# The first store of a pairwise product kernel: issued behind most of the head's loads, or when its products are finished

## The chip, the cores and the metric

The kernel runs on one core of a Trainium2 chip. The metric is the device time of one execution in microseconds (us). The inputs are laid out and the outputs put back in order by the host, which isn't timed.

## The reference

```python
def _L0_rec_ref(x, W):                      # x: 4096 x 32 x 64, W: 64 x 64, float32
    vid = jnp.einsum('bfd,de->bfe', x, W)
    F_ = x.shape[1]
    idx_i, idx_j = jnp.triu_indices(F_, k=1)
    return x[:, idx_i, :] * vid[:, idx_j, :]  # 4096 x 496 x 64
```

For every sample, the 32 fields are multiplied by one matrix, and for each of the 496 pairs of fields i < j the row of field i is multiplied element by element with the transformed row of field j. 33.6 MB go in and 520 MB come out.

## The kernel before

**Tiles and units.** Two halves of the batch lie on the 128 partitions (2 x 64 embedding places), so a tile holds 256 samples: 128 columns for each of 32 fields. There are 16 tiles. All data in on-chip memory stands in one tensor `mem` of 445 units; a unit is 128 columns of float32 on 128 partitions, 64 KB. A tile of x is 32 units, its products are 496 units.

**Work on a tile.** TensorE multiplies the 32 fields by a block diagonal matrix made of W twice (`w2`), in two halves of 16 fields (first fields 16 to 31, then 0 to 15), into `vid`, which fills the PSUM. VectorE then forms the products (L295, `tensor_tensor` with mult), up to 128 pairs in one instruction, from `mem` and `vid` into `mem`. When a half of `vid` is used up it tells TensorE through the semaphore `free`.

**Slots.** The 16 x 496 product units are cut into 74 slots (`SLOTS`), each with a number of units and a home in `mem` where it is gathered, and is then written to `out` by one DMA (`store`, issued through `transfer`, L192). Slots lie over each other and over x data that has been used, so a product instruction waits until the stores that read its place have landed (`after`). Slot 0 has 80 units at 256 to 336, slot 1 109 units at 336 to 445, slot 2 83 units at 240 to 323, slot 3 56 units at 323 to 379. So slot 2 waits for the store of slot 0 to land, and slot 3 for that of slot 1.

**Loads.** x comes in two groups of eight tiles (`GROUPS`). Tile 0 is loaded by two transfers of its own (`first`), the second half of the fields and W ahead. Tiles 1 to 7 come in three pieces, `load(0)`, on the SP queue right behind them: units 96 to 224 (128 units: tiles 1 to 4), 26 to 96 (70 units), 0 to 26 (26 units). Tiles 8 to 15 come in three pieces of 102, 128 and 26 units, `load(1)`, on the ACT queue behind the stores of slots 0 to 36, when the places in `mem` are free. The stores of slots 37 to 73 go through the SP queue.

**Order around the change.** The queues are those of SP and ACT. A DMA is issued when the engine that owns the queue gets through its waits, and later ones stand behind it. `load(g)` returns the semaphores of its three pieces. The variable `hold` keeps them, and the first store that is issued after it (in `store`) waits, beside its own products (`made`), for `hold[-2]`: the last piece but one. This happens twice, for slot 0 and for slot 37. `Queue.waits` leaves out a wait that an engine has already made, directly or through a semaphore that stands behind it.

Of the kernel before, what the change touches and what calls it, by code (L numbers as in the profile page):

```python
# [153 lines left out]
def place_of(t, fields):  # L154

    first = max(begin for begin, _ in GROUPS if begin <= t)
    return TOP - (t - first + 1) * fields


def ends(tiles):  # L160
    return [begin for begin, _ in GROUPS[1:]] + [tiles]
# [6 lines left out]
def pairwise_bilinear_kernel(nc, x0, x, out):  # L168
# [21 lines left out]
    def transfer(out_, in_, units, reads, needs, queue=sp):  # L190
        sem = nc.alloc_semaphore(f"moved{len(moved)}")
        queue.issue(lambda: queue.engine.dma_start(out=out_, in_=in_), needs).then_inc(sem, 16)  # L192
        queue.note(sem, 16)
        moved.append((units, reads, sem))
        return sem

    def after(units):

        needs = [(s, 16) for u, reads, s in moved if reads and overlap(u, units)]
        last = max((n for spans, n in worked if any(overlap(units, s) for s in spans)), default=0)  # L200
        return needs + [(made, last)] * (last > 0)
# [33 lines left out]
    def load(g):  # L235
        (begin, pieces), end = GROUPS[g], ends(NT)[g]
        begin = max(begin, 1)
        low = place_of(end - 1, F)
        sems = []
        for lo, hi in pieces:  # L240
            at = (begin - 1) * F + lo - low
            sems.append(transfer(mem[:, lo:hi, :], x[:, at : at + hi - lo, :], (lo, hi), False, after((lo, hi)), act if g else sp))
            loads.append((range(begin, end), (lo, hi), sems[-1]))
        return sems
# [2 lines left out]
        units = (place_of(t, F), place_of(t, F) + F)  # L247
        return [(sem, 16) for tiles, piece, sem in loads if t in tiles and overlap(piece, units)]

    hold = load(0)  # L250
    begins = [begin for begin, _ in GROUPS]
    held = []

# [13 lines left out]
    for t in range(NT):  # L267
        if t in begins[1:]:
            hold = load(begins.index(t))
# [103 lines left out]
```

How the kernel before makes its waits and increments, by code:

```python
    def issue(self, make, needs):  # L144
        needs = self.waits(needs)
        for sem, n in needs[:-1]:
            self.engine.wait_ge(sem, n)
        instruction = make()
        for sem, n in needs[-1:]:
            instruction.wait_op(sem, n, "sem-ge")
        return instruction
# [16 lines left out]
def pairwise_bilinear_kernel(nc, x0, x, out):  # L168
# [50 lines left out]
            (place + HALF, place + F + 1), False, [],  # L219
        ),
        transfer(mem[:, place : place + HALF, :], x0[:, :HALF, :], (place, place + HALF), False, []),
    ]
    work(lambda: nc.vector.memset(w2[:, :], 0.0), [], [], made)
    for half in (slice(0, D), slice(D, P)):
        work(
            lambda: nc.vector.tensor_copy(w2[half, half], mem[half, place + F, :D]),
            [(place + F, place + F + 1)], [(first[0], 16), (made, 1)], made,
        )
    nc.vector.wait_ge(made, 3).then_inc(free, 1)
    nc.vector.wait_ge(first[1], 16).then_inc(free, 1)
    owed = 0
# [67 lines left out]
            at += n  # L300
            if at == end:
                late = (slot, counts[made])
                group = sum(behind <= slot for behind in STRETCHES)
                if t < begins[group]:
                    held.append(late)
                else:
                    store(*late)
    for sem, n in sp.waits([(sem, 16) for _, _, sem in moved]):
        nc.sync.wait_ge(sem, n)
    def half(xt, lo):
        nc.tensor.wait_ge(free, 1).then_inc(free, -1)
```

## Time and profile before

| what | us |
|---|---|
| median of 3 runs | 1284.41 (1284.06 to 1285.64) |
| profiled execution: span from the first to the last instruction | 1282.9 |
| VectorE busy | 1079.9 (84%) |
| TensorE matmuls busy | 184.4 (14%) |
| DMA queue of SP / of ACT, share of the 16 engines | 50.1% / 49.9% |
| VectorE idle until a store has landed | 113.2 |

The profile is one execution, and times in its rows are counted from the span's start. The median of the runs is 1.5 us above the span: this much lies around it. A DMA is shown by its issue and by the time from issue to landing (the last of its 16 parts is in place); how many bytes all DMA engines move in a stretch is shown as GB/s. In a short stretch that rate is uneven, since a packet counts where it starts.

### The profile page before, as it was taken

To read this page: it belongs to the slowest core of one execution; us is meant where nothing else is said; L and a number is where in the kernel's file an instruction comes from. 1 tells how busy PE (TensorE), PEld (TensorE's weight loads), DVE (VectorE), ACT (ScalarE), POOL (GpSimd) and SP (SyncE) were. 2 spreads that over 40 slices of the span, in tenths; PEclk is the share of its full clock that TensorE was granted. 3 is DMA by queue.
4 is the path that set the end of the run, shared out by engine and by line. 5 is a ranking of instruction groups with operands and counts; after the bars stand their busy time and mean duration, and the time that the engine had idled before them with its cause. 6 is when DMAs were issued, how large, how long until landed. Compare 5 with 4: busy or idle time off the path is not lost. (4 is left out here: it accounts for less than half of the span.)

```text
span 1282.9 us, 1255 instructions
## 1 busy us (share of the span) xinstructions
PE 184.4 (14%) x256; PEld 71.9 (6%) x256; DVE 1079.9 (84%) x273; POOL 0.2 (0%) x4
## 2 busy tenths in 40 slices
PE   2012110302111030300020211103020030202100
PEld 1000000100000010100010000001010010100000
DVE  6589989988897989998028989989998899899980
POOL 0000000000000000000000000000000000000000
PEclk7555565655655565655565565656565565655655
DMA  9999999999999999999999999999999999999999
GB/s 406 424 427 438 435 433 435 443 431 427 437 438 433 425 437 434 436 429 445 418 419 427 436 430 436 438 438 424 440 439 429 432 435 439 425 439 439 431 423 409
DMA packets 11810, 553.70 MB, mean 432 GB/s; under 512 B 1312, under 2 KB 1312, under 8 KB 1312
## 3 DMA queue, kind: packets, MB, share of 16 engines
q1 hardware_dynamic: 6048, 277.38, 50.1%
q10 hardware_dynamic: 5760, 276.30, 49.9%
q14 instruction: 2, 0.02, 0.0%
HBM read 33.59 MB, written 520.09 MB: 432 GB/s over the span
## 5 line engine op out<-in xcount | busy, mean ns | idle before, releaser
L295 DVE TENSOR_TENSOR mem<-mem,vid 128x1024 f32<-128x1024 f32 (+11 forms) x270 | 1079.3, 4065 | 161.5 <-DMA out_dram<-mem 113.2
L315 PE MATMUL vid<-mem,w 128*128 x256 | 184.4, 888 | 1010.2 <-PEq L313 1010.2
L315 PEld LDWEIGHTS vid<-mem,w 128*128 128x128 f32 x256 | 71.9, 295 | 1121.9 <-issue 1121.9
L226 DVE COPY w<-mem 64x64 f32<-64x64 f32 x2 | 0.4, 189 | 5.0 <-DMA mem<-in_r_x_dram 4.9
L223 DVE MEMSET w<- 128x128 f32 x1 | 0.2, 165 | 0.8 <-PEq L340 0.8
L340 POOL MEMSET const-bfloat16-1.0<- 128x1 bf16 x1 | 0.1, 102 | 0.0
L340 POOL MEMSET const-uint8-127<- 128x1 uint8 x1 | 0.1, 102 | 0.0
L340 POOL MEMSET const-float32-0.0<- 128x1 f32 x1 | 0.1, 98 | 0.2 <-issue 0.2
L340 POOL MEMSET const-float32-1.0<- 128x1 f32 x1 | 0.1, 98 | 0.0
## 6 DMA issues: line engine op xcount, KB each, us to landing
out_dram<-mem SPq DMA_DIRECT2D x9, 7680.0 KB, 23.3
out_dram<-mem ACTq DMA_DIRECT2D x3, 7680.0 KB, 23.1
out_dram<-mem SPq DMA_DIRECT2D x3, 7168.0 KB, 21.6
out_dram<-mem ACTq DMA_DIRECT2D x3, 5120.0 KB, 17.5
out_dram<-mem ACTq DMA_DIRECT2D x2, 7168.0 KB, 22.6
out_dram<-mem ACTq DMA_DIRECT2D x2, 6656.0 KB, 21.4
out_dram<-mem SPq DMA_DIRECT2D x2, 6656.0 KB, 19.8
out_dram<-mem ACTq DMA_DIRECT2D x3, 4096.0 KB, 17.5
```

Source lines behind the costliest of these rows:

```text
L223: work(lambda: nc.vector.memset(w2[:, :], 0.0), [], [], made)
L226: lambda: nc.vector.tensor_copy(w2[half, half], mem[half, place + F, :D]),
L295: lambda: nc.vector.tensor_tensor(o, left, right, ALU.mult),
L315: last = nc.tensor.matmul(vid[:, b : b + BANK, :], lhsT=w2[:, :], rhs=xt(b), start=True, stop=True)
L340: nc = _bacc.Bacc("TRN2", target_bir_lowering=False, num_devices=1, dynamic_dma_scratch_size=512)
```

## The change

The wait of the first store for the last load piece but one is taken out; `load(0)` is issued as before, and the wait in front of slot 37 stays. Nothing else is different.

```diff
@@ -247,7 +247,8 @@
         units = (place_of(t, F), place_of(t, F) + F)
         return [(sem, 16) for tiles, piece, sem in loads if t in tiles and overlap(piece, units)]
 
-    hold = load(0)
+    load(0)
+    hold = []
     begins = [begin for begin, _ in GROUPS]
     held = []
 
```

## Rows read from the trace of the kernel before

**Rows 1.** The page: DMA busy tenths in 40 slices, and all that was moved.
```profile
DMA  9999999999999999999999999999999999999999
DMA packets 11810, 553.70 MB, mean 432 GB/s; under 512 B 1312, under 2 KB 1312, under 8 KB 1312
```

**Rows 2.** The waits of VectorE: us in total, times, longest.
```profile
DVE mem L295 <- DMA out_dram<-mem: 113.2, 35, 18.1
```

**Rows 3.** Long stretches: engines' busy us, granted clock, DMA share, GB/s.
```profile
43.80:72.30 28.50, 0.00 (x0) 0.00 (x0) 11.07 (x5) 0.00 (x0) 0.50 1.00 433
72.30:600.00 527.70, 83.47 (x112) 32.22 (x112) 494.90 (x119) 0.00 (x0) 0.57 1.00 434
600.00:684.00 84.00, 9.26 (x16) 3.75 (x16) 24.51 (x8) 0.00 (x0) 0.56 0.99 421
```

**Rows 4.** Head's loads: packets by 2.0 us, issues (start, us), landings (KB, us).
```profile
q1 hardware_dynamic: 12, 0.10, 36.1%
0.73 2.56 SPq L192 DMA_DIRECT2D mem<-in_r_x_dram  x5
mem<-in_r_x_dram SPq DMA_DIRECT2D x1, 1024.0 KB, 7.1
mem<-in_r_x_dram SPq DMA_DIRECT2D x1, 1664.0 KB, 40.9
```

**Rows 5.** First stores, products and matmuls: timeline (start, us); stores' KB, us to landing.
```profile
38.34 0.88 ACTq L192 DMA_DIRECT2D out_dram<-mem  x2
out_dram<-mem ACTq DMA_DIRECT2D x1, 5120.0 KB, 17.5
out_dram<-mem ACTq DMA_DIRECT2D x1, 6976.0 KB, 33.5
13.01 28.00 DVE L295 TENSOR_TENSOR mem<-mem,vid 128x8192 f32<-128x8192 f32 x9 [6.66 <-PE vid L315]
29.34 11.67 DVE L295 TENSOR_TENSOR mem<-mem,vid 128x8192 f32<-128x8192 f32 x4
55.89 11.07 DVE L295 TENSOR_TENSOR mem<-mem,vid 128x1408 f32<-128x1408 f32 x5 [14.88 <-DMA out_dram<-mem]
72.36 62.38 DVE L295 TENSOR_TENSOR mem<-mem,vid 128x1408 f32<-128x1408 f32 x17 [5.39 <-DMA out_dram<-mem]
85.26 6.06 PE L315 MATMUL vid<-mem,w 128*128 x8 [68.93 <-PEq L313]
```

**Rows 6.** DMA packets and queues, 38.4 to 41.6 us, then 41.6 to 44 us.
```profile
DMA packets 76, 1.01 MB, mean 316 GB/s; under 512 B 0, under 2 KB 0, under 8 KB 0
...
DMA packets 55, 1.27 MB, mean 527 GB/s; under 512 B 16, under 2 KB 16, under 8 KB 16
q10 hardware_dynamic: 27, 1.11, 106.5%
q1 hardware_dynamic: 28, 0.16, 18.0%
```

**Rows 7.** The second group's loads: issues, landings, and the first store behind them.
```profile
622.43 1.22 DVE L295 TENSOR_TENSOR mem<-mem,vid 128x1024 f32<-128x1024 f32 x1 [18.09 <-DMA out_dram<-mem]
622.48 1.65 ACTq L192 DMA_DIRECT2D mem<-in_r_x_dram  x2
mem<-in_r_x_dram ACTq DMA_DIRECT2D x1, 55.0
673.77 0.33 ACTq L192 DMA_DIRECT2D mem<-in_r_x_dram  x1
mem<-in_r_x_dram ACTq DMA_DIRECT2D x1, 1664.0 KB, 8.5
678.09 19.88 DMA out_dram<-mem
```

**Rows 8.** Product instructions by shape: busy us, mean ns, idle before.
```profile
L295 DVE TENSOR_TENSOR mem<-mem,vid 128x8192 f32<-128x8192 f32 x1 | 8.7, 8686 | 6.7 <-PE vid L315 6.7
L295 DVE TENSOR_TENSOR mem<-mem,vid 128x2048 f32<-128x2048 f32 x59 | 134.2, 2280 | 10.3 <-DMA out_dram<-mem 10.2
```

## The prediction

> **What bounds the kernel now.** I read the page first. Its DMA line shows a 9 in all 40 slices, for 553.7 MB at a mean of 432 GB/s [rows 1]. VectorE is busy 84%, but its idle time is mostly waiting for stores to free their place: 113.2 us in 35 waits [rows 2]. So the kernel is paced by the bytes that must go through the DMA engines. Then I read long stretches for the rate at which they go. From 72.3 to 600 us it is 434 GB/s; the load of the second group lies lower (600 to 684 us, 421 GB/s) [rows 3]. At 434 GB/s the 553.7 MB take 1275.8 us, against a span of 1282.9. All that any reordering can win is in the 7 us between them, and they can be placed by landings (issue time plus time to landing). A unit is 64 KB (128 partitions x 128 x 4 B), so its transfer takes 0.151 us at 434 GB/s.
>
> - Start: the first two loads, 2080 KB or 4.9 us, are landed at 8.3 us: 3.4 us are gone before and while the first bytes move [rows 4]. The change doesn't touch this.
> - Loads alone: the store that waits for the 70-unit piece is issued at 38.34 [rows 5], so 128 + 70 units take 30.0 us; by the rate 29.9. Nothing is lost. In between, the 128-unit piece must land at 27.6 (an estimate: 8.3 + 128 x 0.151).
> - First change from loads to stores: the last load piece (26 units) and the first two stores (80 and 109 units) land between 38.3 and 72.3 us [rows 4, 5]. That is 215 units, 32.5 us by the rate, and took 34.0: 1.6 us are lost (unrounded). Where: the last load is issued at 2.8, lands 40.9 later, at 43.7 or 43.8; alone it would have been through at 42.2. While the queue of the stores shows not one packet from 38.4 to 41.6 us, the load queue moves only 316 GB/s there [rows 6], and from 43.8 on the rate is 433 again [rows 3].
> - Stores to loads at 622 us: 358 units (a 128-unit store, pieces of 102 and 128 units) land from 622.4 to 677.9, in 55.5 us; by the rate 54.1. 1.4 us lost.
> - Loads to stores again: a 26-unit piece and a 104-unit store land from 677.9 to 698.0, 20.1 us against 19.6: 0.45 us lost [rows 7].
>
> So each change of direction costs 0.45 to 1.6 us of all engines, and pure stretches cost nothing that these rows show.
>
> **The change, part by part.** *Removed:* the first store no longer waits for the 70-unit piece. It was issued at 38.34, its products (80 units) are ready after two instructions that start at 13.01 and take 8.7 and 2.3 us: 23.9 us [rows 5, 8]. So the issue moves 14.4 us forward, to 23.9. It stands at the head of the ACT queue, and ACT has nothing ahead of it; SP's loads were all issued by 3.3 us and are passed by nothing. The second store (109 units) never waited for the loads itself, only behind the first; VectorE makes its last products in the four instructions from 29.34 on, of which the first takes 8.7 us [rows 5, 8], so it is ready after 38.0 in either kernel, and it is issued now 0.5 us after the first, at 38.8 [rows 5]. So exactly one transfer moves. *Added:* nothing but, perhaps, one wait that VectorE inherited through the first store's semaphore and now has to make itself, for a piece that landed hundreds of us earlier: the nearest row is the 17 products from 72.36 on, which pass all their met waits without a gap [rows 5]; I take 0.
>
> *What the earlier store frees.* Its bytes begin about 1.1 us after issue (estimate: the first load is issued at 0.73 and twelve packets have begun by 2.0, the first a little before [rows 4]), say at 25. The loads then still need 13.3 + 3.9 = 17.2 us of the engines. If the two queues share by turns, the store (12.1 us of work) lands 24 us later, at 49 to 50; if loads already queued go first, at 54 or 56. VectorE waits for exactly this landing, from 41.0 to 55.89 us, so it may resume up to 7 us earlier. But its next five instructions take 11.1 us and end at the wait for the second store, at 72.36 [rows 5]. That landing is fixed by the sum of bytes ahead of it, in whatever order. The earlier half of the 14.9 us wait is paid back there: the 5.4 us wait grows to as much as 12. The third store becomes ready at 58 instead of 65.1, still behind the second in its queue. From 72.4 on both kernels are in the same state. The loads that are delayed by this have their cover in the order of the tiles: the matmuls of tile 1 start at 85 us [rows 5], its data is in the 128-unit piece, which lands a few us after 27.6 at worst, and the two smaller pieces (the smallest as late as about 70 instead of 43.8) hold tiles 5 to 7. If that cover were gone, each us of lateness would be one of PE and VectorE, and one of the DMA engines only when no finished store is left in the queue.
>
> *What can change the end* is therefore only the number of us in which the engines move less than 434 GB/s before 72.4, and such a loss, or a gain, passes through to the end unchanged, since the engines are never without work after it.
>
> - The old direction change at 39 to 43 us, 1.6 us, no longer happens as it was: -1.6.
> - A new one happens at 25 us, with stores joining running loads, and one when the loads run out. Bounds by the rows of the three changes seen: 0.45 for one such change to 1.6 + 1.4 for both of them. I take 1.0 for all, between the two changes from loads to stores that the trace has, since this is the same kind.
> - A mixed stretch is added: 17 us if loads go first, some 45 us if packets of the two queues alternate one for one to the end of the small load packets (each piece is 128 rows, 8 an engine, so 16 packets for the two smaller pieces, each followed by one of a store of 12.1 / 8 = 1.5 or 16.5 / 8 = 2.1 us). No row shows two queues with much work each. Bounds: nothing (by the 433 of the unmixed stretches), and 14% of 45 us, 6.3 us, by the loss of 0.45 us in the 3.1 us in which both queues had work, 679.2 to 682.3 [rows 7]. I take 0.3, by the rows of pure stretches, since what the trace shows of a loss is bound to the few us around a change and not to work on two queues.
>
> Sum: -1.6 + 1.0 + 0.3 = -0.3 us on a span of 1282.9, so 1282.6; the median of the runs lies 1.5 us above the span (1284.4), so 1284.1.
>
> On whether the store gets its turn at all, the trace shows that no packet of the store's queue is counted until every engine has nearly finished its load packets, 3.3 us after the issue [rows 6]. The Trainium skill ("DMA: Bandwidth & Descriptors", section Queues, rings and completion order) says that each engine takes turns between its queues, packet by packet. By that rule the store lands at about 50 us; read straight from the trace, at about 55. The sum of the bytes is the same by both, but by the rule rival B below has 45 us to act in, by the trace 17.
>
> On the price of mixing, the same page (section Latency and other measured facts) gives 214 GB/s in each direction at once for copies of large tiles, 428 together. By it, an estimate, 45 mixed us would cost 0.6 us, against my 0.3; no run here shows it.
>
> **The rivals.**
>
> *A, nothing moves.* The engines work off what is queued, so the store issued at 23.9 starts after the last load packet as now. For it: where a store is issued beside loads now, the loads' packets come first [rows 6]. Against it: at 38.4 the loads had 76 + 28 packets left less 16 under 512 B, 5 or 6 small ones an engine; here it would be 17. Then the span stays: 1284.4. VectorE's wait would still end at 54 to 56.
>
> *B, slower: mixing costs in every us, not per change.* The place is the stretch from 25 us until the loads are through; the mechanism is that an engine which turns from a load packet to a store packet and back loses part of each turn. For it: 316 GB/s against 434 in the stretch 38.4 to 41.6, in which the store was issued and the loads weren't through [rows 6], so 27% lost; at 679 to 682 14%. Against it: in the head the loss is over by 43.8 us [rows 3], and 1.4 us are also lost after 622 us, where one queue alone holds stores and loads in order [rows 7]. Price: with 14% over 45 us 6.3 - 1.6 = +4.7 us, 1289.1; with 27% over 45 us 12.2 - 1.6 = +10.6, 1295.0. It decides the sign from a loss of (2.6 + 1.6) / 45 = 9% on, below that it is no change that can be seen.
>
> *C, faster.* Loads and stores use opposite directions of the memories and together exceed 434 GB/s. It would take 10% more over 45 us to gain 4.5 + 1.6 us, 1278.3. Against it: no stretch of the trace, mixed or not, holds more than 434 over a longer time [rows 3]. Without it the gain ends at 1.6 us, 1282.8.
>
> **How the numbers follow.** About 0.2% (2.6 us) is what a measurement of this kernel can tell from no change, so forecast and A both count as the same. Forecast 0.45, 1284.1 with its own range 1282.6 to 1286.5; A 0.25, 1284.4; B 0.26, of which a third lies under 1289.5, the rest up to 1300 and over; C 0.04. Faster by over 0.2%: 0.04. Slower: B with loss over 9%, 0.24 and a remainder of the forecast's own upper bound, 0.01, so 0.25. Same: 0.71. For eight in ten the range takes forecast and A whole and the lower part of B, with C left out below: 1282.4 to 1290.
>
> **What would show it.** The store's issue at about 23.9 on ACT. VectorE's first wait for a store ending at 49 to 56 instead of 55.89, and the next still ending at 72 within 2 us: later than 74 is B, and by as much as the whole time grows; before 71 it is C. The GB/s of 25 to 45 us: near 434 the forecast, 370 or less B. From there on every landing is shifted by one constant. The prediction is wrong if the landing at 72 moves by more than 2.6 us, or if the shift isn't kept to the end, for then the engines had idle time that I haven't seen.

## The result, and the profile after

The changed kernel takes 1289.59 us (1288.03 to 1290.8, 5 runs) against 1284.41: ratio 1.0041, interval [1.003, 1.0052]. It is slower by 5.2 us by the medians, 0.4%. The profiled execution is one of 1288.03 with a span of 1286.7, 3.8 over the span of before (1282.9). This is the fastest of the five executions. A later profile of the same kernel (e2_after_again, below), of an execution of 1289.98, has a span of 1288.7, 5.8 over before, so both are used.

The page of after: span, 40 slices of DMA share and GB/s, and all that was moved; to be held against [rows 1].
```profile
span 1286.7 us, 1254 instructions
DMA  9999999999999999999999999999999999999999
GB/s 386 425 428 430 431 443 432 444 424 424 439 442 424 434 429 449 416 452 428 422 426 414 428 432 437 434 441 424 435 440 434 432 433 439 429 432 434 436 425 407
DMA packets 11810, 553.70 MB, mean 430 GB/s; under 512 B 1312, under 2 KB 1312, under 8 KB 1312
```
The GB/s of before, slice by slice:
```profile
GB/s 406 424 427 438 435 433 435 443 431 427 437 438 433 425 437 434 436 429 445 418 419 427 436 430 436 438 438 424 440 439 429 432 435 439 425 439 439 431 423 409
```
The same packets and bytes move at 430 instead of 432 GB/s. The first slice (32 us) has 386 instead of 406, which is 1.5 us' worth of transfers; in the others the differences go both ways, by up to 23. So the page says that the loss is in the transfers and that a part of it is made in the first 32 us, and not where the rest is. That is told by VectorE's waits for landed stores, since each ends with a landing. The timeline of after (start, us busy, instructions; in brackets the idle time before and what ended it), first the issues of the first three stores on ACT, then VectorE:
```profile
23.59 37.69 ACTq L192 DMA_DIRECT2D out_dram<-mem  x3
51.69 11.08 DVE L296 TENSOR_TENSOR mem<-mem,vid 128x1408 f32<-128x1408 f32 x5 [11.02 <-DMA out_dram<-mem]
74.28 27.61 DVE L296 TENSOR_TENSOR mem<-mem,vid 128x1408 f32<-128x1408 f32 x7 [11.51 <-DMA out_dram<-mem]
150.86 5.95 DVE L296 TENSOR_TENSOR mem<-mem,vid 128x1408 f32<-128x1408 f32 x2 [2.48 <-DMA out_dram<-mem]
625.66 1.22 DVE L296 TENSOR_TENSOR mem<-mem,vid 128x1024 f32<-128x1024 f32 x1 [18.48 <-DMA out_dram<-mem]
701.66 4.89 DVE L296 TENSOR_TENSOR mem<-mem,vid 128x384 f32<-128x384 f32 x2 [6.42 <-DMA out_dram<-mem]
```
Two of these rows have partners of before that are not among the rows ahead:
```profile
149.01 5.95 DVE L295 TENSOR_TENSOR mem<-mem,vid 128x1408 f32<-128x1408 f32 x2 [2.55 <-DMA out_dram<-mem]
698.00 13.48 DVE L295 TENSOR_TENSOR mem<-mem,vid 128x384 f32<-128x384 f32 x3 [6.08 <-DMA out_dram<-mem]
```
The first store is issued at 23.59 (the second goes out at 38.4, 0.4 us before its time in the kernel before), and VectorE's first wait ends at 51.69 instead of 55.89 [rows 5]. It gives that back: the next wait is 11.5 us instead of 5.4 and ends at 74.28 instead of 72.36, 1.9 later. At 149 us the two kernels are 1.85 apart, at 622 us 3.2 (625.66 against 622.43 [rows 7]), at 698 us 3.7, at the end 3.8. The delay isn't made in one place: a half of it in the head, over a third in the long stretch in which nothing but stores moves, the rest at the second group.

The long stretches, to be held against [rows 3] (us, busy us of PE, PEld, DVE, POOL, granted clock, DMA share, GB/s):
```profile
43.80:72.30 28.50, 0.00 (x0) 0.00 (x0) 11.08 (x5) 0.00 (x0) 0.50 1.00 412
72.30:600.00 527.70, 84.27 (x112) 32.89 (x112) 492.09 (x118) 0.00 (x0) 0.56 1.00 433
600.00:684.00 84.00, 8.72 (x16) 3.60 (x16) 24.02 (x8) 0.00 (x0) 0.56 1.00 424
```
412 instead of 433 GB/s in the first, with the engines busy all the time (share 1.00 in both). The second has 433 for 434: in GB/s a loss of 1.4 us is hardly visible, it takes landings to see it.

One reading is used for the head in all that follows. A queue's MB divided by the share of its packets' time, by 16 and by the window is the rate of an engine while it is busy for that queue. A packet counts in the window in which it starts, with its bytes and with its whole time, so the edges of a window don't falsify this rate. It is 27.1 GB/s undisturbed (434 / 16); what is missing to that, times the share and the window, are us lost per engine. The DMA queues of after (q1 is SP's with the loads, q10 is ACT's with the stores; packets, MB, share of 16 engines) from 24 to 30, 30 to 46 and 54 to 70 us:
```profile
q1 hardware_dynamic: 40, 1.44, 78.7%
q10 hardware_dynamic: 18, 0.74, 28.4%
...
DMA packets 182, 6.84 MB, mean 428 GB/s; under 512 B 3, under 2 KB 3, under 8 KB 3
q1 hardware_dynamic: 99, 3.44, 49.7%
q10 hardware_dynamic: 83, 3.40, 49.1%
...
DMA packets 172, 5.99 MB, mean 374 GB/s; under 512 B 0, under 2 KB 0, under 8 KB 0
q10 hardware_dynamic: 87, 4.86, 77.2%
q1 hardware_dynamic: 85, 1.13, 16.5%
```
- When the store joins, the loads' packets go at 19.0 GB/s: 6 x 0.787 x (1 - 19.0 / 27.1) = 1.4 us lost per engine. The same reading of before, 38.4 to 44 us, gives 0.8 (its row is with e1). The slowed packets are the loads' own, and they lie ahead of the store's: from 24 to 28 us not one packet of the store's queue starts, the first does at 28.5, 4.9 us after the issue. From then to 46 us the store's packets are at full speed.
- From 30 to 46 us 99 packets stand against 83, at 27.0 GB/s each way: the queues take turns, and it costs nothing.
- From 54 to 70 us they still take turns, the second store's packets against small load packets, and these store packets go at 24.6 GB/s: 1.1 us lost per engine. From 46 to 54 us, read the same way, it is 0.2.

1.4 + 0.2 + 1.1 - 0.8 = 1.9, which is what the landing at 72.3 is late by. But a landing is that of the slowest of 16 engines, and these figures are means of all, so such an agreement isn't to be counted on: see e2.

### The profile page after: what moved, and what is told of

It is laid out like the page before. It is cut to its first block, busy times and chain, and to the rows that moved or that the text cites. A ratio compares the mean times of both kernels' runs of the same rounds, so it can differ in the third digit from the quotient of the medians.

```text
span 1286.7 us, 1254 instructions
## 1 busy us (share of the span) xinstructions
PE 185.9 (14%) x256; PEld 72.7 (6%) x256; DVE 1079.9 (84%) x273; POOL 0.2 (0%) x4
## 4 chain that ended last, share of the span: by engine, by line
another core or an unknown queue 53%; DVE 25%; DMA 18%; issue 2%; SPq 0%
DVE mem L296 25%; DMA out_dram<-mem 18%; SPq L192 0%; SPq L147 0%
```

## Experiments

Each run stood beside runs of the kernel before on the same chip, 1284.13 to 1284.48 us by the median. The runs were made on four chips: e1 to e4 on one, e5 to e8 on the second, e9 to e12 on the third, e13 to e16 on the fourth. The stages of all are put together in a table behind them.

**The two kernels again.** No edit.

> The kernel before, unchanged, for a second trace. It tells how much of the difference between the two traces is the change and how much is one execution against another. In the first trace 1.5 us were lost to the full rate of the engines by the end of the head (5.1 us lag at the landing of the second store, 3.4 of them from the start), and 0.5 us more grew until 604 us. If that slow growth belongs to the kernel, the same 0.5 us is seen again; if it varies from execution to execution, it lies anywhere up to the 1.8 us seen in the trace of after. Time: 1284.4 within 1.5 us.

> The changed kernel again. Theory 1 (the cost is in the head alone: 1.4 us where the store joins the running loads, and 0.33 us in each of six turns between a 26-unit load packet and a 109-unit store packet): the second store lands at 74.3 us again, 1.9 us later than before, and what comes after 74 us is chance. Theory 2 (the head leaves the engines in a worse order, which costs a further 1 us on the way to 604 us): the lag grows by 1.5 to 2 us from 74 to 604 us again. Theory 3 (every us of mixing costs): the stretch 30 to 49 us, in which 70-unit load packets and 80-unit store packets take turns, would show less than 434 GB/s; the first trace of after shows none of that. Time: 1289.5 within 1.5 us.

Before again: 1284.34, ratio 1.0 [0.9991, 1.0009]. After again: 1289.98, 1.0042 [1.0028, 1.0056]. The head loses more this time: the landing is at 75.7, 3.4 over before. The queues of before from 38.4 to 44 us, then q10 of e2 from 54 to 70 us:
```profile
q1 hardware_dynamic: 104, 1.17, 63.1%
```
```profile
q10 hardware_dynamic: 94, 5.25, 83.6%
```
The first is 20.7 GB/s, so 5.6 x 0.631 x 0.24 = 0.8 us lost per engine. The second is 24.5 GB/s, 1.3 us. With 1.4 for the join and 0.2 from 46 to 54 us, e2 lost 1.4 + 0.2 + 1.3 - 0.8 = 2.1 of its 3.4 us on the mean of the engines; the rest is a lag of the slowest one, and no row places it. The stretch from 149 to 622 us is as long as in after (474.78 and 474.79; before 473.42 and 473.49): that part of the loss repeats closely, the head's part spreads.

**Are the small load packets what makes the turns slow?** The two small pieces made one of 96 units, and then the pieces cut smaller.
```diff
-    (0, [(96, 224), (26, 96), (0, 26)]),
+    (0, [(96, 224), (0, 96)]),
```


> The changed kernel, with the 70-unit and the 26-unit piece of the head as one load of 96 units. No small load packets are left, so only 8 turns of the two queues, 96-unit against 80-unit packets, and the loads are through before or as the second store begins. Theory 1: the join at 24 us still costs 1.4 us, the turns nothing, so the second store lands about 72.3 to 72.8 us and the time is 2 us under after: 1287.5, or 1285 if all that is lost later comes from the head. Theory 3, or a fixed price for each turn whatever its packets: half of the turns go, so half of the extra time at least stays, 1287 and the landing at 73.3 or later with slow packets between 30 and 50 us. If nothing in the mixing matters: 1289.5.

```diff
-    (0, [(96, 224), (26, 96), (0, 26)]),
+    (0, [(96, 224), (52, 96), (26, 52), (0, 26)]),
```


> The changed kernel, with the 70-unit piece cut into 44 and 26 units, so that 16 small load packets per engine (26 units) stand against stores instead of 8. Bytes are the same. Theory 1 (a small load packet before a large store packet costs 0.33 us on most engines): up to 8 turns more, 2 to 2.6 us more than after, 1292, and the landing of the second or third store is later by this. A price for each turn whatever its size: the same direction, but turns against 80-unit packets would be slow as well. If the packets' size plays no part: 1289.5.

> The kernel with two small load pieces a second time. Its six executions took 1286.5 to 1291.7 us, and the one with a trace, the fastest, had not one slow turn. If slow turns are what makes the others long (theory 1, now: turns run at full speed or at 0.3 us a round, which of the two being a matter of the execution), a trace of an execution of 1290 or more shows 20 or more slow store packets between 45 and 85 us, and the third store lands 2 us or more later; a trace of one of 1286 to 1287 shows none. If the long ones have no slow turns, the head isn't what makes them long.

Merged: 1287.63, 1.0023 [1.0014, 1.0032]. Smaller: 1290.31 (1286.47 to 1291.73), 1.0044 [1.003, 1.0058], about as slow as after. A second look at that kernel: 1288.77 in one run. q10 of e3 from 36 to 54 us, then of e4 and of e13 from 54 to 70 us:
```profile
q10 hardware_dynamic: 80, 3.28, 50.7%
```
```profile
q10 hardware_dynamic: 120, 5.46, 78.8%
```
```profile
q10 hardware_dynamic: 110, 5.10, 76.4%
```
In e3 the stores' packets go at 22.5 GB/s against large load packets, 1.6 us lost per engine: slow turns don't need small ones, and that cause falls. Why e3 is all the same 2 us faster than after by the medians, its profile doesn't tell (the span is 0.5 us shorter). e4 and e13 are one kernel on two chips: in the first execution, its fastest, the packets go at 27.1 GB/s, in the second at 26.1. VectorE, resuming when the third store has landed, in e4 and e13:
```profile
84.70 6.55 DVE L296 TENSOR_TENSOR mem<-mem,vid 128x6144 f32<-128x6144 f32 x1 [1.55 <-DMA out_dram<-mem]
```
```profile
87.12 6.55 DVE L296 TENSOR_TENSOR mem<-mem,vid 128x6144 f32<-128x6144 f32 x1 [1.84 <-DMA out_dram<-mem]
```
2.4 us later, and the span is 2.3 us longer (1287.5 against 1285.2). So whether turns are slow differs between executions of one program, here on different chips, and it accounts for the difference of these two. That it makes the whole spread of the kernel's times (1286.47 to 1291.73 on the one chip) isn't shown, with one profile of each. Turns can run at full speed; what decides it none of the runs shows.

**Which stores have to leave the loads alone?** The first two stores, only the first, or only the second put behind the loads on the SP queue, on the kernel after.
```diff
-        transfer(rows[:, : end - begin, :], mem[:, units[0] : units[1], :], units, True, needs, act if slot < STRETCHES[0] else sp)
+        transfer(rows[:, : end - begin, :], mem[:, units[0] : units[1], :], units, True, needs, act if 2 <= slot < STRETCHES[0] else sp)
```


> The changed kernel, with the first two stores issued through the SP queue, behind the loads, instead of through ACT. The first is still issued at 23.9 us and waits for no load, but the two queues have nothing to take turns with before the third store. If the cost of the change is the sharing of the engines by two queues in opposite directions (theory 1: join and turns), it is gone: the second store lands at 72 us, there is one change of direction at 42 us in the queue itself, and the time is that of before, 1284.2, or up to 1 us less. If the early issue itself costs (the descriptors of a second transfer while loads run), it stays at 1286 or more.

```diff
+        transfer(rows[:, : end - begin, :], mem[:, units[0] : units[1], :], units, True, needs, act if 1 <= slot < STRETCHES[0] else sp)
```


> As the last, but with only the first store in the SP queue; the second goes through ACT at 38.8 us, when its products are ready. From 40 to 42 us loads and a store take turns, from 42 to about 66 us two stores. If turns cost whatever the direction, 8 rounds of 0.33 us are paid and it takes about 1287. If they cost only where loads and stores meet, 1284.2 to 1285.5.

```diff
+        transfer(rows[:, : end - begin, :], mem[:, units[0] : units[1], :], units, True, needs, act if slot != 1 and slot < STRETCHES[0] else sp)
```


> The changed kernel, with the second store (109 units) in the SP queue behind the loads. The first store still joins the running loads through ACT and takes turns with them; the turns of small load packets with 109-unit store packets, where the traces of after show nearly all of their slow packets, are gone, and no two queues are busy together after 50 us. If those turns are the loss after the join (1.2 us on the mean, 2 us on the slowest engine), 1287 to 1288; if the loss is in the join and the drift, 1289.5 as after.

Measured: both 1285.78, 1.0013 [1.0004, 1.0022]; the first 1297.26, 1.0101 [1.0085, 1.0116]; the second 1289.99, 1.0044 [1.003, 1.0057].

e5 takes away what after loses more than before in the head, read by landings: the third store lands at 84.72 (before 84.87). The change of direction inside its one queue still costs: the packets started from 38.4 to 44 us, loads and stores together, move 2.24 MB in 112.1% of the window, which is 1.1 us lost per engine. But from 149 to 622 us it takes 474.79, like after. So the long stretch's loss isn't left over from slow turns in the head.

e6 was the surprise. VectorE's wait, the 9 us behind it (us, busy us, clock, DMA share, GB/s), and the queues from 44 to 70 us:
```profile
72.21 23.41 DVE L296 TENSOR_TENSOR mem<-mem,vid 128x1408 f32<-128x1408 f32 x8 [30.75 <-DMA out_dram<-mem]
```
```profile
72.30:81.50 9.20, 0.00 (x0) 0.00 (x0) 9.20 (x4) 0.00 (x0) 0.50 0.00 0
```
```profile
q10 hardware_dynamic: 117, 6.53, 57.9%
q1 hardware_dynamic: 112, 4.59, 40.8%
```
Two stores on two queues take turns too, at 27.1 GB/s (6.53 / (0.579 x 16 x 26)) and 27.0, so here turns in one direction cost nothing. But both then land at 72.2 and 72.3 instead of one at 56. VectorE needs the first one's place and stands still for 30.75 us, and when both land no finished store is left: the engines move 0 GB/s for 9 us. The order of the landings costs 11 us (the ninth store lands at 159.88, in e5 at 148.80). e12 has the milder form: the second store shares with the third and lands at 82.2, VectorE waits 18.4 us, and from 82 to 90 us only 148 GB/s move. So e12 is as slow as after for a reason of its own, and can't say what the second store's turns cost.
```profile
82.00:90.00 8.00, 0.00 (x0) 0.00 (x0) 7.80 (x3) 0.00 (x0) 0.50 0.34 148
```

**Does the moment of the join decide?** On the kernel before, the first store waits for the last piece, or for the first piece only (27 us).
```diff
-            needs.append((hold[-2], 16))
+            needs.append((hold[-1 if slot == 0 else -2], 16))
```


> The kernel before, with the first store waiting for the last load piece instead of the last but one: it is issued at 42.2 us. No load meets a store. The engines stand idle for the time from issue to first bytes, about 1.3 us. If the 0.8 us that each engine loses on average between 38 and 44 us in before (1.6 us on the slowest) comes from loads and stores in the engines at once, no packet is slowed here, and idle time of 1.3 us takes its place: 1284.2 within 1 us. If the loss comes with the change of direction as such, it is paid beside the idle time: 1285.5.

```diff
+            needs.append((hold[-3 if slot == 0 else -2], 16))
```


> The kernel before, with the first store waiting for the first load piece (128 units, landed at 27.6 us), 3.7 us later than in after, 10.7 us earlier than in before. All turns of after but one are still there (8 of 70 against 80 units, 8 of 26 against 109 units). Theory 1: nearly all of the loss of after, 1288 to 1290. If what counts is the meeting with the 128-unit packets (the slow packets of the join), or the wait for x data in flight, it falls back to 1284.5 to 1286.

> The kernel whose first store waits for the first load piece, a second time: its executions took 1284.3 to 1287.6, the one with a trace 1286.5, with no slow turn, a second store landed at 72.2 as in before, and 2.1 us more than before at the loads of the second group. Theory 1 expects either no slow turn and at most 1287.6, or slow turns and a landing after 73.5. What the second group costs is expected to differ between the two looks, if it is a matter of how the engines stand when they get there.

Last piece: 1286.79, 1.0019 [1.001, 1.0028]. First piece: 1285.58, 1.001 [1.0001, 1.0019]; again in one run, 1285.38. The head of e7 from 42 to 44 and from 44 to 72 us, and VectorE behind it:
```profile
42.00:44.00 2.00, 0.00 (x0) 0.00 (x0) 0.00 (x0) 0.00 (x0) 0.50 0.78 328
44.00:72.00 28.00, 0.00 (x0) 0.00 (x0) 11.08 (x5) 0.00 (x0) 0.50 1.01 434
```
```profile
149.47 13.48 DVE L295 TENSOR_TENSOR mem<-mem,vid 128x1408 f32<-128x1408 f32 x3 [2.90 <-DMA out_dram<-mem]
624.54 1.22 DVE L295 TENSOR_TENSOR mem<-mem,vid 128x1024 f32<-128x1024 f32 x1 [18.50 <-DMA out_dram<-mem]
```
With no store beside a load, no packet is slowed; an idle gap takes its place (share 0.78), and the landing is all the same at 72.43 as before (72.33). Yet the stretch takes 475.07 instead of 473.42. (Not all of this is lost in the stretch. The trace has the time of each of the 16 parts of a landing: by their mean the ninth store lands at 149.35 in e7 and at 147.90 in before, 1.45 us apart, where the last parts are 0.5 apart; and by the mean the stretch is 1.0 us longer, not 1.65.) In e8 and e14 (one kernel on two chips) the store joins at 28 us, for 1.2 us lost per engine, and the turns of loads and stores all run at full speed; the second stores land at 72.24 and 71.99, and the stretch takes 473.95 and 474.04, nearly as before. q10 of e8, 54 to 70 us, 27.1 GB/s:
```profile
q10 hardware_dynamic: 112, 6.25, 90.1%
```
So the early join by itself doesn't make the landing at 72 late. But the second group takes 77.7 and 76.7 us in these two, against 75.6.

**What is it in the long stretch?** The engines start their packets either spread over time or in bursts. GB/s in 40 slices of 0.25 us, from 296 to 306 us, before, then e7:
```profile
GB/s 262 0 0 786 1835 0 524 0 786 262 0 0 0 1311 1311 0 524 524 262 262 0 0 262 1835 524 524 0 786 0 262 0 0 1049 1573 0 524 0 786 262 0
```
```profile
GB/s 0 0 786 3146 0 262 0 0 0 0 0 0 1835 2097 0 262 0 0 0 0 0 0 3670 262 262 0 0 0 0 0 0 524 3408 0 262 0 0 0 0 0
```
A slice counts the packets that start in it. Before they start in two groups and some singles, with few gaps; in e7 nearly all 16 start within 0.5 us and then nothing for 1.5. After lies between, and closer to e7:
```profile
GB/s 0 0 0 0 0 0 1311 1049 1311 524 0 0 0 0 0 0 1835 1049 1049 262 0 0 0 0 0 262 1835 1311 786 0 0 0 0 0 0 1311 1311 1049 524 0
```
A theory followed: engines that start together get in each other's way, and each packet takes a little longer. To spread them, one transfer between places in device memory was added on a few engines only, into bytes of `out` that slot 20's store overwrites later (the store waits for it). The same addition on e7's kernel, on after and on before:
```diff
+    rest = BLOCKS[20]
+    extra = transfer(
+        out[rest : rest + 8 * 64, :].rearrange("(p u) c -> p u c", p=8), x[:8, :64, :], (0, 0), False, [(first[1], 16)], act
+    )
```


> The kernel in which the first store waits for the last load piece, with one transfer more: 8 rows of 32 KB from one place in device memory to another, issued at 8 us through ACT, which occupies 8 of the 16 engines for about 1.2 us each and nobody reads. In the trace without it the engines run in step from 42 us on, and each packet between 100 and 600 us takes 0.1 to 0.3% more than it must, about 1.4 us in all; in executions whose engines are spread over a packet's time it is 0.3 us. If running in step is the cause (theory 2), the extra transfer puts half of the engines half a packet apart, and the loss from 100 to 600 us falls to 0.9 us or less, against up to 1.2 us paid at the start by 8 engines: 1286 to 1288. If the drift is only chance, it stays at 1.4 and the time goes to 1288.0.

> The changed kernel with the same extra transfer. In its traces the slow turns (a store packet of 2.06 us takes 2.4) were seen on the 11 to 13 engines that turned at the same moment, and not on the 3 to 5 others. If turning in step is the cause, half of the engines are moved by half a turn, slow turns become few, and the time is that of after less 1 to 2 us, plus up to 1.2 us for the transfer itself: 1287.5 to 1290 with few slow packets from 50 to 72 us. If the step plays no part, slow turns stay on 11 or more engines and 1.2 us are added: 1291.

> The kernel before with the same extra transfer: its price where there is nothing to mend, since the engines there are spread already by the change of direction at 40 us. 8 engines lose 1.2 us, and if these are the slowest ones in the end the time is 1285.4; if the change of direction takes it up, 1284.2.

1287.81, 1.0026 [1.0016, 1.0036]; 1289.98, 1.0043 [1.0029, 1.0056]; 1285.73, 1.0011 [1.0002, 1.002]. The stretch takes 474.91, 474.78 and 474.02. In e10 the slow turns stay as well (1.1 us per engine, 50 to 70 us). In e9 the offsets didn't last: the store's wait for the last piece lines the engines up again behind them, so it shows nothing about the theory. e10 and e11 do. In e10 the engines start spread at 296 to 306 us, about as in before, and the stretch is as long as that of after:
```profile
GB/s 262 0 0 1573 524 786 0 0 1049 0 262 0 0 2097 262 524 0 786 262 0 262 0 0 2097 524 262 0 1049 0 262 0 0 1573 524 786 0 0 1049 0 262
```
In e11 the extra transfer made the stretch of before longer, by 0.6 us. The same was then done late on e7's kernel, behind slot 4's store, in one size and in four.
```diff
+        if slot == 4:
+            rest = BLOCKS[20]
+            for n, u in ((8, 64), (4, 32), (2, 16), (1, 8)):      # e15: ((8, 64),)
+                extra.append(transfer(
+                    out[rest : rest + n * u, :].rearrange("(p u) c -> p u c", p=n), x[:n, :u, :], (0, 0), False, [], act
+                ))
+                rest += n * u
```


> The kernel whose first store waits for the last load piece, with the extra transfer on 8 engines issued at 87 us, behind the fifth store, where nothing lines the engines up again. In e9 the later wait for the last piece lined them up, and the trace was in step again at 300 us. From the landing of the ninth store to the resuming of VectorE at 622 us it takes 473.4 us in before, 475.1 in e7 and 474.9 in e9. If running in step costs, two groups half a packet apart bring it under 474.5; if not, it stays at 475. The time: 1286.8 and up to 1.2 more for the transfer.

> As the last, with four extra transfers on 8, 4, 2 and 1 rows (64, 32, 16 and 8 units of 512 B a row), so that the engines stand up to a packet's time apart: the slowest is 2.2 us later at the ninth store. If the in-step loss is the whole difference between e7 and before, the same stretch takes 473.5 to 474; if spreading isn't what helps, 475.

One run each: 1288.58 and 1289.16. The transfers cost 2.0 and 3.5 us of their own by the ninth store (151.47 and 152.94, e7 149.45), but behind it the stretch shrinks from 475.07 to 474.58 and 473.75, the second of which is as short as with e8's spread. GB/s of e16 from 296 to 306 us, and VectorE:
```profile
GB/s 786 262 0 0 0 262 2621 262 0 524 262 262 0 0 0 786 2097 262 0 786 262 0 0 0 262 2359 524 0 0 786 262 0 0 0 524 2359 262 0 524 262
```
```profile
152.96 5.95 DVE L303 TENSOR_TENSOR mem<-mem,vid 128x1408 f32<-128x1408 f32 x2 [3.58 <-DMA out_dram<-mem]
626.71 1.22 DVE L303 TENSOR_TENSOR mem<-mem,vid 128x1024 f32<-128x1024 f32 x1 [18.09 <-DMA out_dram<-mem]
```
The head was the same, only the order among the engines was changed, and by landings 1.3 us of the 475.07 came back. But both ends of the stretch are the times of one engine, and the extra transfers hold up some engines more than others just ahead of it: the parts of the ninth store land within 0.2 us in e7 and within 2.8 us in e16. By the mean of the 16 parts the stretch takes 473.8 us in before, 474.8 in e7, 474.6 in after, 474.9 in e10 and 474.3 in e16, so the transfers gave back a half of the 1.0 us between e7 and before. That is all that speaks for the theory, in one execution. Against it stand e10, spread and slow, and e14, whose stretch is short with bursts about as wide as after's:
```profile
GB/s 0 0 0 0 0 1573 786 1049 524 262 0 0 0 0 262 1573 1049 1049 0 262 0 0 0 0 786 1049 1573 524 262 0 0 0 0 0 1573 786 1049 524 262 0
```

**The stages of all.** Landings of the second store, of the third and of the ninth (VectorE's resume less 0.02), then the us between the landings for which VectorE waits at about 149 (in e5 and e12, where it doesn't wait there, the ninth landing itself), 622 and 698, and from there to the last landing.

| kernel | 2nd store | 3rd | 9th | 149 to 622 | 622 to 698 | to the last landing | span |
|---|---|---|---|---|---|---|---|
| before | 72.33 | 84.87 | 148.98 | 473.42 | 75.57 | 584.95 | 1282.9 |
| e1, before | 72.04 | 84.60 | 148.70 | 473.49 | 75.61 | 585.17 | 1283.0 |
| after | 74.26 | 86.61 | 150.84 | 474.79 | 76.01 | 585.05 | 1286.7 |
| e2, after | 75.71 | 88.08 | 152.33 | 474.78 | 76.61 | 584.92 | 1288.7 |
| e3 | 73.66 | 86.23 | 150.34 | 474.82 | 75.95 | 585.03 | 1286.2 |
| e4 | 68.51 | 84.67 | 149.04 | 474.39 | 77.07 | 584.64 | 1285.2 |
| e13, as e4 | 70.64 | 87.09 | 151.18 | 474.65 | 76.83 | 584.77 | 1287.5 |
| e5 | 75.28 | 84.72 | 148.80 | 474.79 | 75.29 | 585.42 | 1284.3 |
| e6 | 72.34 | 95.44 | 159.88 | 474.99 | 75.97 | 585.23 | 1296.1 |
| e12 | 82.18 | 86.87 | 155.31 | 475.25 | 75.81 | 585.28 | 1291.7 |
| e7 | 72.43 | 85.06 | 149.45 | 475.07 | 76.20 | 585.28 | 1286.0 |
| e8 | 72.24 | 84.79 | 148.89 | 473.95 | 77.71 | 584.64 | 1285.2 |
| e14, as e8 | 71.99 | 84.53 | 148.66 | 474.04 | 76.71 | 584.63 | 1284.1 |
| e9 | 73.63 | 86.25 | 150.70 | 474.91 | 75.71 | 585.30 | 1286.6 |
| e10 | 75.74 | 88.13 | 152.40 | 474.78 | 76.36 | 584.90 | 1288.5 |
| e11 | 72.53 | 85.08 | 149.21 | 474.02 | 75.86 | 585.30 | 1284.4 |
| e15 | 72.48 | 85.07 | 151.47 | 474.58 | 75.89 | 585.30 | 1287.3 |
| e16 | 72.49 | 85.09 | 152.94 | 473.75 | 75.46 | 585.66 | 1287.8 |

Twelve of the eighteen profiles lie between 474.4 and 475.3 us in the long stretch, six between 473.4 and 474.1. Two profiles of one kernel lie within 0.3 us of each other in this stretch (before and e1, after and e2, e4 and e13, e8 and e14), also on different chips, so its length goes with the kernel more than with the execution. No version beat the kernel before.

## Why the prediction was wrong

It gave 1284.1 with 0.71 for no change; it came out 1289.6, slower, which it gave 0.25. That 1289.6 lies in its range of 1282.4 to 1290 is owed to the part of rival B that was taken into it; the forecast's own range ended at 1286.5. The step that failed is the sum -1.6 + 1.0 + 0.3 = -0.3 us, with its premise that only these terms can change the end: the head came out at +1.9 us (e2: +3.4), and another 1.9 (e2: 2.4) came behind it, where the sum has no term. Step by step:

- *The issue moves to 23.9.* Right: 23.59. SP's loads aren't passed, and but for 0.4 us of the second store exactly one transfer moves.
- *The store lands at 49 to 50 if the queues take turns, at 54 or 56 if not.* Turns: VectorE resumes at 51.69, and 99 against 83 packets are counted from 30 to 46 us. It is 2 us later than by that sum, which had the first bytes at 25 and no price for the join; the first packet starts at 28.5. This is what the Trainium skill says ("DMA: Bandwidth & Descriptors", section Queues, rings and completion order), each engine taking turns packet by packet; here the trace agrees (99 against 83). Rival A, in which nothing moves, is out: that no store packet was counted for 3.3 us [rows 6] belongs to the join (4.9 us in after) and not to an order of loads first.
- *The first wait's gain is paid back at the second.* Right: 14.9 falls to 11.0 us, 5.4 rises to 11.5 ("as much as 12"). That the late load pieces are covered was right too: the end moves only by what the engines lost. e6 shows what this cover hangs on, a finished store left in the queue.
- *The landing at 72.3 is fixed by the sum of bytes.* Wrong by 1.9 us (e2: 3.4), and the two small terms of the sum were at fault. "1.0 for all" changes of direction: the join alone costs 1.4 us per engine, where the old change, counted the same way, cost 0.8; I had read it as 1.6, by the landing of the slowest engine, and taken all of that off. And "0.3" for the mixed stretch: 30 to 46 us cost nothing, but the slow turns later cost 1.3 us (0.2 + 1.1), in e2 1.5. The upper bound of 6.3 us held them.
- *Pure stretches cost nothing; a loss passes to the end unchanged.* Wrong, and with this the list of where anything could change was wrong: +1.4 us from 149 to 622 us and +0.4 to 1.0 at the second group, together a half of what was lost in after (e2: two fifths). I had the rate of one stretch of one execution [rows 3] and took it for a property of the chip. Why the stretch is longer none of the runs shows. e5 shows this most plainly: its ninth store lands within 0.5 us of before's, by the last part (148.80) as by the mean of the parts (148.41 against 147.90), and it is still slower. e7 shows it by the last part only.
- *Rival B, mixing costs in every us* had the sign, and by 1289.1 nearly the time, and the prediction's own sign for it, a landing later than 74, was met, narrowly (74.28; e2 75.7). Its mechanism, each turn losing a part, acts in a part of the stretch only: it is seen from 46 to 70 us, where the store's packets go at up to 9% under the full rate, and not from 30 to 46, where the turns run at 27.0 GB/s; those of e4, e8 and e14 run at full speed throughout. With 14% in each of 45 us the landing at 72.3 would have moved by 4.7, not by 1.9, and over a third of the whole loss lies where nothing but stores moves, so that B came near the time is luck. The price of 14% came from a change of direction, not from turns.
- *Rival C, more than 434 GB/s with both directions at once* is out: 428 GB/s at 30 to 46 us, and 374 at 54 to 70 us. The 214 GB/s per direction, for which the prediction named the same page of the Trainium skill (section Latency and other measured facts), are given there for copies between tensors in HBM, which are read and written there; here a byte crosses HBM once. So the 428 of 30 to 46 us doesn't confirm that figure, and the 374 doesn't contradict it.

Of the prediction's own signs, "from there on every landing is shifted by one constant" was the one that told: 1.9, 3.2, 3.7, 3.8 us.

What stays open: what decides in an execution whether turns between loads and stores are slow; what makes the long stretch 1.4 us longer (engines in step alone don't: e10 is spread and slow, e14 in bursts and fast); and why the second group takes 75.3 to 77.7 us.

## What to carry to other kernels

In a kernel whose DMA engines are never idle, look whether moving a store forward among loads can free anything: here the wait that got shorter was made up at the next one, and what remained was the price of the join and of the turns. Follow the shift between two kernels from landing to landing up to the end, and profile the kernel before twice, ahead of calling a rate fixed. Before work is split over two queues, ask whose place is needed first: sharing delays the older transfer's landing, and that may leave the engines with nothing to move.

## What was not expected of the hardware

- A store that joins running loads costs 1.2 to 1.4 us of each engine (after, e8), more than the change of direction with the loads nearly through (0.8) and about as much as stores behind loads in one queue (1.1, e5). The slowed packets are the loads', ahead of the store's first one.
- Turns between loads and stores run at 27.1 GB/s per engine or at 22.5 to 24.6, and one program does either in different executions, here on two chips (e4 and e13). Turns between two stores ran at full speed (e6).
- The same stores on one queue took from 473.4 to 475.3 us for the stretch from the ninth store on, depending on what the kernel did ahead of it.
